# Cross-attention with image-prompt tokens on one core: the output projection of a batch moved from four visits behind odd pairs to two visits behind the values of pairs 6 and 8

## The reference

```
q = split_heads(x @ w_q);  k, v from the 248 text rows with w_k, w_v
out_text = softmax(q k^T / 4) v
k_ip, v_ip from the 8 special rows with w_k_ip, w_v_ip
out_ip = softmax(q k_ip^T / 4 + mask_ip(bbox)) v_ip
out = (out_text + out_ip) @ w_out + b_out + x
```

## Time and profile before

| | |
|---|---|
| median of three runs | 549.91 us (546.61 to 556.17) |
| time of the profiled execution | 547.39 us |
| its span, first to last instruction | 545.6 us |
| around the span | 1.8 us |
| TensorE busy | 479.0 us (88% of the span) |
| VectorE busy | 387.4 us (71%) |
| ScalarE busy | 275.6 us (51%) |
| GpSimd busy | 134.8 us (25%) |
| mean granted TensorE clock | 0.958 |

### The profile page before, as it was taken

How to read it: one execution, slowest core, us unless ns; L and a number is a source line. 1 busy time by engine, 2 the same in 40 slices (tenths; PEclk the granted TensorE clock), 3 DMA queues, 4 the chain that set the end, 5 groups by cost and what they waited for, 6 DMA issues and landing times.

```text
span 545.6 us, 11048 instructions
## 1 busy us (share of the span) xinstructions
PE 479.0 (88%) x4304; PEld 323.1 (59%) x4304; DVE 387.4 (71%) x706; ACT 275.6 (51%) x355; POOL 134.8 (25%) x206
## 2 busy tenths in 40 slices
PE   3969017799999999999999999999999999798895
PEld 2858016557666676667665766667566765455442
DVE  2733614868797778787797778777878779799832
ACT  3632001356665466545565565555664556566670
POOL 7013000004220313231422223130503131423441
PEclk9989658899999999999999999999999999999997
DMA  8988096485947777685859394948667565483011
GB/s 280 364 287 145 13 311 232 120 261 186 334 143 231 238 245 257 159 288 159 270 183 338 94 335 137 311 146 299 201 195 269 170 224 167 169 264 113 9 51 48
DMA packets 93956, 112.50 MB, mean 206 GB/s; under 512 B 14304, under 2 KB 72672, under 8 KB 93904
## 3 DMA queue, kind: packets, MB, share of 16 engines
q1 hardware_dynamic: 92960, 109.57, 62.5%
q0 software_dynamic: 944, 2.23, 2.4%
HBM read 73.17 MB, written 38.63 MB: 205 GB/s over the span
## 4 chain that ended last, share of the span: by engine, by line
issue 54%; POOL 21%; PE 9%; DMA 7%; DVE 6%; SPq 3%; ACT 1%; POOLq 0%; ACTq 0%; DVEq 0%
POOL o_turned L402 9%; POOL o_all L407 7%; POOL x_all L396 4%; DMA probs<-in_wv_ip 3%; DVE max_cols L558 2%; DMA v_rows<-v_out 1%; PE score_q L685 1%; PE score_q L645 1%; DMA q_stack<-aux_rows 1%; DVE x_all L514 1%; PE score_q L647 1%; PE score_q L646 1%; PE pj L757 1%; PE pv L748 1%; DMA raw<-in_xT 1%
## 5 line engine op out<-in xcount | busy, mean ns | idle before, releaser
L558 DVE TENSOR_REDUCE max_cols<-score_q 128x4 fp32r<-128x992 f32 x160 | 189.0, 1181 | 100.1 <-PE score_q L685 99.6
L483 ACT ACTIVATE probs<-score_t 128x1024 f32<-128x1024 f32 x160 | 163.4, 1021 | 142.4 <-PE score_t L734 142.3
L748 PE MATMUL pv<-probs,v_cur 128*32 128x256 f32 x1920 | 120.2, 383 | 0.6 <-ACT probs L483 0.6
L402 POOL TENSOR_TENSOR o_turned<-o_turned,inv_cols 128x256 f32<-128x256 f32 x80 | 53.9, 674 | 148.4 <-DVE inv_cols L601 148.2
L757 PE MATMUL pj<-wo_sb,o_all 128*128 128x320 f32 x192 | 70.6, 478 | 9.5 <-DVE out_sb L613 5.6
L748 PEld LDWEIGHTS pv<-probs,v_cur 128*32 128x32 f32 x1920 | 54.3, 109 | 39.0 <-issue 1.0
L396 POOL TENSOR_TENSOR x_all<-x_all,bias_sb 128x640 f32<-128x640 f32 x16 | 24.9, 1558 | 199.9 <-DMA x_all<-in_x 199.9
L685 PE MATMUL score_q<-k_stack,q_stack 64*128 64x256 f32 x440 | 46.3, 289 | 30.7 <-DMA q_stack<-aux_rows 23.1
L598 DVE STREAM_TRANSPOSE o_turned<-o_all 128x512 f32<-128x512 f32 x80 | 55.9, 699 | 11.8 <-ACT o_all L475 11.8
L734 PE MATMUL score_t<-q_stack,k_stack 64*128 64x256 f32 x440 | 55.5, 330 | 7.3 <-ACT probs L483 5.4
L475 ACT ACTIVATE o_all<-pv 128x512 f32<-128x512 f32 x80 | 47.8, 598 | 27.4 <-PE pv L748 27.4
(11 more groups left out here) (147 smaller groups left out, 635.5 us busy)
## 6 DMA issues: line engine op xcount, KB each, us to landing
k_stack<-k_parts SPq DMA_DIRECT2D x33, 320.0 KB, 5.1
q_stack<-q_parts SPq DMA_DIRECT2D x33, 320.0 KB, 6.7
v_rows<-v_out SPq DMA_DIRECT2D x32, 320.0 KB, 4.6
v_cur<-v_rows SPq DMA_DIRECT2D x16, 640.0 KB
q_parts<-qk_out SPq DMA_DIRECT2D x32, 256.0 KB, 3.2
k_parts<-qk_out SPq DMA_DIRECT2D x32, 248.0 KB, 6.2
raw<-in_ctxT SPq DMA_DIRECT2D x14, 512.0 KB, 5.1
x_all<-in_x SPq DMA_DIRECT2D x16, 320.0 KB, 7.5
```

What stands on the lines that cost most here:

```text
L402: pool.tensor_tensor(out, out, inv_cols[:, n % SLOTS, :].unsqueeze(2).broadcast_to([P, 2 * S // 32, DH]), ALU.mult).then_inc(scaled, 1)
L483: nc.scalar.activation(probs[:, slot(t % 2, p), :], score_t[:, :], ACT.Exp, scale=SCALE)\
L558: nc.vector.tensor_reduce(out=max_cols[:, h, :, at:at + 4:2].rearrange("p t e -> p e t"), in_=both[:, :, :, 0:TEXT], op=ALU.max, axis=AX.X ...
L748: last = mm(pv[32 * t:32 * t + 32, at:at + S], values_of(u, kind, 4 * k + t), probs[:, slot(u, 2 * k + t // 2), a:a + S], start=kind != 1, ...
```

## The change

`project_out` loses its chunk argument and does all three chunks of one output tile in one visit. The visits stand in pairs 6 and 8, behind the values of these pairs. The residual is added in pairs 7 and 9 of the same batch; so the second tile is finished one step of the loop earlier than before. Line 640, the last `finish`, is no longer needed.

```diff
-            finish(B - 1, OT - 1)
...
-            def project_out(b, t, c):
-                if t == 0:
-                    pe.wait_ge(o_ready, OC * b + c + 1)
-                if c == 0:
-                    need(pe, out_done, OT * b + t)
-                last = mm(pj[:, 0:D], o_norm[:, b % 2, c, t * P:t * P + P], wo_sb[:, c, :],
-                          start=c == 0, stop=c == OC - 1)
-                if c == OC - 1:
-                    last.then_inc(out_ready, 1)
+            def project_out(b, t):
+                need(pe, out_done, OT * b + t)
+                for c in range(OC):
+                    if t == 0:
+                        pe.wait_ge(o_ready, OC * b + c + 1)
+                    last = mm(pj[:, 0:D], o_norm[:, b % 2, c, t * P:t * P + P], wo_sb[:, c, :],
+                              start=c == 0, stop=c == OC - 1)
+                last.then_inc(out_ready, 1)
...
-                    for m, k in OUT.get(p, ()):
+                    for m in OUT.get(p, ()):
                         if there(t - 1):
-                            project_out(t - 1, m, k)
+                            project_out(t - 1, m)
...
-OUT = {3: [(0, 0), (0, 1)], 5: [(0, 2)], 7: [(1, 0), (1, 1)], 9: [(1, 2)]}
-FINISH = {6: [(0, -1)], 0: [(1, -2)]}
+OUT = {6: [0], 8: [1]}
+FINISH = {7: [(0, -1)], 9: [(1, -1)]}
```

## The result

The changed kernel takes 567.51 us (median of four runs, 567.11 to 573.33); four runs of the kernel before on the same chip have a median of 551.22. The ratio is 1.0349, with a 95% interval of 1.0241 to 1.0457: slower by 3.5%, where 562.8 us (2.8% above the profiled execution) had been forecast, and inside the forecast range. Ratios in this text are of executions in the faster of two states in which the kernel runs, and so they aren't quotients of the medians. The profiled execution took 567.88 us, its span 566.1 us, 20.5 more than before.

What follows compares the result with a forecast made beforehand. TensorE was taken to bound hosted batches, and a loop of key scores, exponential, values and PSUM copy those without tiles. Profiled 547.4 + 6.6 (hosted) + 8.8 (without tiles) = 562.8 us; range 552 to 571.

Steps and rivals of the forecast that it cites:

- The price of a visit: TensorE, behind values of pairs 6 and 8: three chunks cost 1.81 us, a batch 3.62, 0.38 more than before.
- Rival 2: Visits: no gap behind three chunks, 1.62 us each; 5.3 us less than forecast, so 557.5 us, +1.8%; chance 0.09.
- The waits removed: TensorE's projection waits for `finish` (0.39 us each) and the turn back (0.34) go, together 1.12 us per two batches.
- Short odd pairs in hosted batches: Batches 1 to 10: VectorE loses the projection's cover, stalls form; 1.32 us per mean double batch, +6.6 us for five.
- gaps behind four visits: Hosted double batch: visits ahead of key scores cost a 0.20 us gap more than ahead of a tile; +0.76 us.
- first stall of an even batch: Query scores of pair 1 wait for VectorE's maxima of pair 0: a new stall of 0.63 us.
- second stall, query scores of pair 6: Even hosted batches: TensorE waits at pair 6 for VectorE's maxima of pair 5, a stall of 0.79 us.
- later `x` at pair 5: Even hosted batches: a later `x` load lengthens the second stall by as much, 0.26 us per mean double batch.
- the sentence that let TensorE reach pair 1 at 279.03: Batch 6: TensorE would be at pair 1's query scores at 279.03 but, needing the maxima, starts about 279.66, 0.62 late.
- Batches without tiles: Batches 12 to 15: visits delay odd pairs' key scores and exponential; +0.4, +2.3, +2.7, +3.4, together +8.8 us.
- Rival 4: Hosted batches: later turns and loads delay `x` further, 1.7 to 2.5 us per double batch, 568 us; chance 0.08.
- Start and tail: Time up to batch 1 and after the last values: forecast difference 0; the tail keeps its order.

Runs made afterwards that it cites:

- e5_odd_pairs: Changed kernel with its two three-chunk visits moved to pairs 7 and 9, ahead of the tile and behind the scores; 550.42 us, ratio 0.9968.
- e7: Kernel before with its four visits; first residual add moved from pair 6 to 5, last turn back from pair 4 to 3; 548.07 us, ratio 0.9858.
- e4_ctx_before_rows: Changed kernel with the load of the second half of `ctx` issued ahead of the load of the row maxima; 570.38 us, ratio 1.0348.
- e1: Kernel before with the change's two visits only from batch 12 on, the old four visits in batches up to 11; 559.42 us, ratio 1.0154.
- e9_turn_first: Changed kernel with the turn in pairs 4 and 9 issued directly behind the maxima of that pair; 564.18 us, ratio 1.0221.
- e3_second_finish_later: Changed kernel with the second residual add put back from pair 9 to pair 0 of the next batch; 567.25 us, ratio 1.0286.
- e2_hosted_only: Kernel before with the change's two visits only in batches up to 11, the old four visits from batch 12 on; 563.65 us, ratio 1.0213.

## Why the prediction was right, and where it was not

The direction, the two places of the loss and, but for one wait, their mechanisms were right, and both losses were taken too small: 19.0 us in the stages that the change touches, where 15.4 had been forecast. The medians differ by only 16.3 us; that this is so near to the forecast is in part luck.

**The price of a visit: right.** 1.81 us behind values, and 1.61 ahead of a tile in `e5_odd_pairs`; the gap of 0.20 belongs to the key scores behind the projection. Rival 2, three chunks without a gap, would have 1.62 and is out. The section "Back-to-back issue gap" of the Trainium skill's page "TensorE: Matmul & The Clock Gate", whose formula for a matmul by itself has no charge for a change of neighbour, agrees with the visit ahead of a tile and falls short by about 0.2 of the one ahead of key scores (1.63 by its figures, an estimate).

**The waits removed: right, and each worth a little more than its idle time.** Idle 0.39 and 0.34 us had been put down for them, 1.12 per double batch. Pair 7 of an odd batch, 4.26 us, less the same pair without a chunk (2.71) and two chunks (1.08), leaves 0.47; an even one 0.44; pair 5 of an even batch 0.48: 1.39. e7, which removes the waits alone, gives 0.47, 0.44 and 0.42.

**"Short odd pairs in hosted batches": the term that was too small.** Forecast +1.32 per double batch, measured 9.1/5 = 1.82. By the lengths of the pairs after, per double batch:

| step | forecast | measured |
|---|---|---|
| gaps behind four visits | +0.76 | +0.76 |
| waits removed | -1.12 | -1.39 |
| first stall of an even batch | +0.63 | +1.34 |
| second stall, query scores of pair 6 | +0.79 | +0.81 |
| later `x` at pair 5 | +0.26 | +0.42 |

The sum of the right column is 1.94; the 0.12 that is left is of the size of what pairs differ among themselves, and of a wait for the exponential that the kernel before already had once (batch 9, 0.44). The second stall is where it was forecast and as long: 0.93, 0.95, 0.70, 0.94 and 0.55 in the five even batches. The first is twice as long and, in four of five, a pair earlier: 1.33, 0.93, 1.46 and 1.62 at the key scores of pair 0, and 1.13 at pair 1 in batch 2, with 0.21 more at pair 1 of batch 6. The step that failed is the sentence that let TensorE reach pair 1 at 279.03: it counted VectorE and left out ScalarE, whose exponential of pair 9 stands behind the split of `ctx`, already 0.1 us from being the last. In batch 5 the load is 0.90 us later, and without its stall the batch would be 0.15 us shorter than before (27.46 and 27.61); less the 0.1 to spare that makes 0.95, and pair 9 grew by 0.93. `e4_ctx_before_rows` shows that the forecast stall lies behind it: without the late load it comes at pair 1 with 1.14. So only 0.20 of what the first stall has above 0.63 is the load. The other 0.51 comes with VectorE, and most of it is the second thing that this step left out: it took L534 at its old length, and 0.36 is what L534 then waits for GpSimd, since `finish` lets L402 begin first. For the 0.15 that is left no cause is shown.

**"Batches without tiles": right, and 1.1 us too small.** +0.9, +2.4, +3.1 and +3.5 us in batches 12 to 15, forecast +0.4, +2.3, +2.7 and +3.4. The loop of two pairs, forecast 5.53, is 5.54 and 5.62 in batch 14, and 5.35 was 5.30 and 5.40 in batch 15. The 0.25 taken off batch 14 as an estimate was there (pair 3 goes from 1.94 to 1.70), but pair 0, which had been left out, grew by 0.27 (2.10 to 2.37). e1, which has this change alone, shows the same +9.8.

**Rival 4**, the `x` chain that feeds on itself at 1.7 to 2.5 per double batch, has the size (1.82) but not the mechanism: the later `x` is 0.42 of it, and 0.25 of the second stall goes with it in `e9_turn_first`, where `x` is early; the sum stays there only because the load of `ctx` takes longer.

**Start and tail** were put at nothing and came out at +3.4 and -1.8 in these two executions: the first arises ahead of any changed instruction, the second goes with the granted clock.

Left open: why the load of `ctx` took 5.9 to 6.8 us from issue to split in two batches of `e9_turn_first` (and 6.58 in batch 5 of `e3_second_finish_later`), where it took 4.0 to 5.1 in the changed kernel; how much of the first stall, beyond the 0.36, is the earlier second `finish`, for which the times of `e3_second_finish_later` are too coarse; and the 2.9 us at the end of `e2_hosted_only`.

## What to carry to other kernels

In programs of several in-order engines, work on one engine is also cover for the lateness of another: the same twelve matmuls cost 3.5% more in even pairs ahead of key scores and nothing that the times can tell in two visits behind the scores of odd pairs. Where an engine waits for another, move the releaser rather than the work that waits: two table entries moved on VectorE removed the same waits and gained 1.4% (0.9 to 1.9). And before a step is moved, list on every engine what is within some tenths of a microsecond of being late, loads behind queue entries included; here one load with 0.1 us to spare stood in front of the stall that had been worked out, and that stall was itself longer, because a step put in ahead of a VectorE operation let GpSimd go first.

## What the runs showed of the hardware

Two things had not been expected. A VectorE subtraction of two SBUF operands (L534, 128x1024) and GpSimd's operations L396, L402 and L407 hold each other up, and the one that begins later waits. In the twelve profiles, from 100 us on, each L534 that began with 0.15 us or more of such an operation still to run ended 1.07 to 1.10 us behind that operation's end, and so took up to 2.53 us (batch 7 of the changed kernel), where it takes 1.16 to 1.23 otherwise. Where L534 began first, L402 ended 0.47 to 0.49 us behind its end and L407 0.31 to 0.33, whole lengths from 1.3 to 1.7 us where they take 0.62 and 0.46 by themselves. The Trainium skill, "SBUF — State Buffer", section "Who interferes with whom", names just this pair as one that contends (two SBUF inputs on VectorE, a GpSimd operation that reads SBUF); the traces agree. And the float32 matmuls of the projection are followed by a gap of 0.20 us if the next matmuls are the 64-row key scores (1.81 us for a visit), and by none that shows ahead of the 128-row tiles (1.61 to 1.66).
